# One sparse and one global attention stage of an eight-stage kernel: biases, rotary halves, row sums and start order moved between engines

## The reference

```python
# sparse, over the 2048 tokens
Q, K, V = (x @ W.T + b for each)            # 16 heads of 8
q_scores = 0.5*l2 + 0.3*entropy + 0.2*var   # of each row of Q, softmax over its 8 elements
_, top_idx = jax.lax.top_k(q_scores, 10)    # 10 queries a head
attn = softmax(Q_sparse @ K.T / sqrt(8)); out = attn @ V      # rows beyond u are dropped
return full.at[top_idx].set(out) @ Wo.T + bo
# global: 16 heads of 64, 4 key and value heads
q = q * cos + _rotate_half(q) * sin;  k = k * cos + _rotate_half(k) * sin
attn = softmax(q @ k.T * 64**-0.5);  out = attn @ v
return out @ Wo + bo
```

## Time and profile before

| | us |
|---|---|
| median of 3 runs (range) | 3885.16 (3882.11 to 3892.41) |
| the profiled execution, its own time | 3877.67 |
| its span, first to last instruction | 3875.9 |
| mean granted clock | 0.945 of full |
| busy in the span: PE, DVE, ACT, POOL | 3460.4, 2522.3, 1832.9, 1613.7 |

### The profile page before, as it was taken

How to read it: one execution, slowest core, us unless ns; L and a number is a source line. 1 busy time by engine, 2 the same in 40 slices (tenths; PEclk the granted TensorE clock), 3 DMA queues, 4 the chain that set the end, 5 groups by cost and what they waited for, 6 DMA issues and landing times. The chain is left out here.

```text
span 3875.9 us, 61610 instructions
## 1 busy us (share of the span) xinstructions
PE 3460.4 (89%) x23550; PEld 2161.1 (56%) x23550; DVE 2522.3 (65%) x4730; ACT 1832.9 (47%) x3269; POOL 1613.7 (42%) x1100
## 2 busy tenths in 40 slices
PE   6999999999857647999669999999999999978997
PEld 4777787878756435777523333333333333336776
DVE  4565656565655456777567777677677766757776
ACT  2344444434323124999423334333433333339997
POOL 1212121111104123666225556556655666656664
PEclk9999999999988557999879999999999999989999
DMA  2000000000010001000100000000000000010000
GB/s 94 1 1 1 1 1 1 1 1 1 1 45 9 6 0 44 2 2 2 38 0 1 1 1 1 1 1 1 1 1 1 1 1 1 1 44 2 2 2 12
DMA packets 21486, 31.46 MB, mean 8 GB/s; under 512 B 8418, under 2 KB 17932, under 8 KB 19724
## 3 DMA queue, kind: packets, MB, share of 16 engines
q1 hardware_dynamic: 21196, 27.52, 2.3%
HBM read 26.46 MB, written 1.05 MB: 7 GB/s over the span
## 5 line engine op out<-in xcount | busy, mean ns | idle before, releaser
L3027 POOL TENSOR_TENSOR global_acc_pool<-global_acc_pool,global_probs 128x1024 f32<-128x1024 f32 x320 | 776.7, 2427 | 470.6 <-ACT global_probs L2980 452.6
L2980 ACT ACTIVATE global_probs<-global_ps 128x1024 f32<-128x1024 f32 x512 | 524.7, 1025 | 883.2 <-PE global_ps L2853 856.9
L3075 DVE TENSOR_REDUCE global_part<-global_ps 128x2 f32<-128x1024 f32 x512 | 624.7, 1220 | 428.9 <-PE global_ps L2835 428.7
L2853 PE MATMUL global_ps<-global_q,global_k 64*128 64x512 f32 x2048 | 522.4, 588 | 0.0
L2864 PE MATMUL global_ps<-global_probs,global_v 128*64 128x512 f32 x2048 | 495.7, 605 | 0.0
L2835 PE MATMUL global_ps<-global_khh,global_qhh 64*128 64x512 f32 x1024 | 324.9, 631 | 35.9 <-DVE global_part L3075 33.9
L994 DVE COPY_PREDICATED delta_Y<-delta_tri,delta_ps 128x512 f32<-128x512 uint32 x192 | 140.4, 731 | 290.9 <-PE delta_ps L533 290.9
L900 POOL TENSOR_TENSOR delta_gm<-C_tile,delta_g 128x1024 f32<-128x1024 f32 x16 | 30.4, 1897 | 718.9 <-PE delta_ps L453 685.3
L2851 PE MATMUL global_ps<-global_mrow,global_first 64*128 64x512 f32 x1024 | 323.6, 629 | 0.0
L2864 PEld LDWEIGHTS global_ps<-global_probs,global_v 128*64 128x64 f32 x2048 | 124.3, 136 | 282.6 <-issue 161.4
L2835 PEld LDWEIGHTS global_ps<-global_khh,global_qhh 64*128 64x128 f32 x1024 | 97.9, 188 | 323.0 <-DVE global_part L3075 259.3
(11 more groups left out here) (587 smaller groups left out, 6862.3 us busy)
## 6 DMA issues: line engine op xcount, KB each, us to landing
delta_cw<-in_conv_taps SPq DMA_DIRECT2D x4, 1024.0 KB, 11.5
local_tab<-in_rot_tables SPq DMA_DIRECT2D x2, 2048.0 KB, 12.3
local_tab<-in_rot_tables SPq DMA_DIRECT2D x2, 1536.0 KB, 7.9
localw_wqkv<-in_L_ffn_wqkv SPq DMA_DIRECT2D x2, 768.0 KB
delta_wqkvz<-in_L_attn_a_W_qkvz SPq DMA_DIRECT2D x1, 1024.0 KB, 6.5
local_tab<-in_rot_tables SPq DMA_DIRECT2D x2, 512.0 KB, 4.2
global_cos<-in_rope_cos SPq DMA_DIRECT2D x2, 512.0 KB, 10.2
global_sin<-in_rope_sin SPq DMA_DIRECT2D x2, 512.0 KB, 11.7
```

Source lines behind the costliest of these rows:

```text
L2853: mm = pe.matmul(ps[:, 2 * (at % 2) + s, :], k2[own, group_of(u) % 2, P * k:P * k + P], q[own, u % 3, :], start=False, stop=True)
L2980: act.activation(probs[:, at % RING, :], ps[:, 2 * (at % 2):2 * (at % 2) + 2, :].rearrange("p b n -> p (b n)"), ACT.Exp).then_inc(S["probs ...
L3027: ins = eng.tensor_tensor(sums[:, u % 2, :], sums[:, u % 2, :], probs[:, at % RING, :], ALU.add)
L3075: dve.tensor_reduce(part[:, u % 2, r % SLOTS, :], ps[:, 5:7, :], X_AXIS, ALU.max)\
```

## The change

In the sparse stage the bias matmuls go, and DVE adds the biases of q and v while it copies them out of PSUM; ACT squares the copy; PE transposes a group ahead of each projection; the exponentials are interleaved with the copies. In the second block the probabilities stay unscaled, both halves are transposed before one series of 16 matmuls with 160 columns, and the inverse sums scale the output rows in the ACT copy.

In the global stage a rope key has one projection. ACT copies its halves of 32 partitions crosswise out of PSUM, with the sign (`swap_halves`, four activations of 32x512), and DVE multiplies the projection by cosine and the swapped copy by sine. The weights are loaded during the local stage before, the tables in four parts with a semaphore each. The first rope keys are interleaved with the rough scores of unit 0, which use two pairs of banks. POOL adds the two partial sums (`merge_sums`), so that `out_sums` has two matmuls for four. `out_sums`, the inversion, `out_rows` and the adding of rows each come one span later; POOL adds the output bias.

```diff
@@ -1819,21 +1819,20 @@
-                    def project(g, banks, i, bias):
+                    def project(g, banks, i):
                         for t in range(GROUP):
-                            own = ps[:, banks[g % 2], P * t:P * t + P]
-                            pe.matmul(own, xnT[:, g % 2, P * t:P * t + P], wT[:, i, :], start=True, stop=False)
-                            mm = pe.matmul(own, ones[0:1, :], bias[0:1, :], start=False, stop=True)
+                            mm = pe.matmul(ps[:, banks[g % 2], P * t:P * t + P], xnT[:, g % 2, P * t:P * t + P], wT[:, i, :],
+                                           start=True, stop=True)
                         return mm
...
+                    turn_rows(0)
+                    pe.wait_ge(S["wT_ready"], 1)
                     for g in range(GROUPS):
-                        turn_rows(g)
-                        if g == 0:
-                            pe.wait_ge(S["wT_ready"], 1)
+                        if g + 1 < GROUPS:
+                            turn_rows(g + 1)
                         project_all(g)
@@ -1867,24 +1867,26 @@
+                    def exponents(g):
                         act.wait_ge(S["shifted"], g + 1)
                         act.activation(e8[:, g], e8[:, g], ACT.Exp).then_inc(S["exp_ready"], 1)
+
+                    keep_rows(0)
+                    for g in range(GROUPS):
+                        if g + 1 < GROUPS:
+                            keep_rows(g + 1)
+                        keep_projections(g)
+                        if g:
+                            exponents(g - 1)
+                    exponents(GROUPS - 1)
@@ -1911,12 +1913,20 @@
+                        tiles = slice(GROUP * g, GROUP * g + GROUP)
+                        dve.wait_ge(S["q_ps"], g + 1)
+                        dve.tensor_tensor(q_all[:, tiles, :], ps[:, Q_BANKS[g % 2], :].rearrange("p (t d) -> p t d", t=GROUP),
+                                          over_middle(bq, GROUP), ALU.add).then_inc(S["q_ready"], 1)
+                        dve.wait_ge(S["v_ps"], g + 1)
+                        dve.tensor_tensor(v_all[:, tiles, :], ps[:, V_BANKS[g % 2], :].rearrange("p (t d) -> p t d", t=GROUP),
+                                          over_middle(bv, GROUP), ALU.add).then_inc(S["v_ready"], 1)
@@ -2003,28 +2013,27 @@
-                def contexts(g):
-                    pe.wait_ge(A["probsT_ready"], g + 1)
+                def contexts():
+                    pe.wait_ge(A["probsT_ready"], 2)
                     for t in range(TILES):
-                        mm = pe.matmul(ps[:, 4 * g + 3, 0:HALF], v_all[:, t, :], probsT[:, g, t, :],
+                        mm = pe.matmul(ps[:, 7, 0:H * TOP], v_all[:, t, :], probsT[:, :, t, :],
...
                 turn_probs(0)
-                contexts(0)
                 turn_probs(1)
-                contexts(1)
+                contexts()
@@ -2050,7 +2059,8 @@
-                    act.activation(ow[:, g, :], ps[0:HALF, 5 + g, 0:DIM], ACT.Copy).then_inc(A["ow_ready"], 1)
+                    act.wait_ge(A["weights_ready"], g + 1)
+                    act.activation(ow[:, g, :], ps[0:HALF, 5 + g, 0:DIM], ACT.Copy, scale=srow[:, g:g + 1]).then_inc(A["ow_ready"], 1)
@@ -2105,12 +2115,11 @@
                     link(dve.reciprocal(own, own))
-                    link(dve.tensor_tensor(own, own, valid[:], ALU.mult))
-                    dve.tensor_scalar(probs[:, g, :], probs[:, g, :], own, None, ALU.mult).then_inc(A["probs_ready"], 1)
+                    dve.tensor_tensor(own, own, valid[:], ALU.mult).then_inc(A["weights_ready"], 1)
...
-                own_heads(1)
+                row_weights(0)
+                row_weights(1)
+                dve.wait_ge(A["o_ps"], 1)
+                dve.tensor_tensor(oT[:], heads(ps[:, 7, 0:H * TOP], H), over_inner(hm, TOP), ALU.mult)\
...
+                load_global_weights(sp, C)
 
             @block.tensor
...
 
-    rope_order = [("k", 0, b) for b in range(QB)] + [("q", 0), ("q", 1)]
+    rope_order = [("q", 0)] + [("k", 0, b) for b in range(QB)] + [("q", 1)]
     for u in range(UNITS):
@@ -2787,52 +2829,56 @@
+                for b in range(QB):
+                    cols = slice(BLK * b, BLK * b + BLK)
+                    for half in (UP, DOWN):
+                        sp.dma_start(cos[half, cols], W["rope_cos"][:, cols]).then_inc(tables[b], 16)
+                        sp.dma_start(sin[half, cols], W["rope_sin"][:, cols]).then_inc(tables[b], 16)
+                sp.dma_start(wo[:], W["L1_attn_b_Wo"].rearrange("(c p) n -> p c n", p=P)).then_inc(S["wo_loaded"], 16)
...
-                pe.matmul(ps[:, 7, :], weights, xnT[:, cols], start=True, stop=True).then_inc(S["proj_ps"], 1)
+                    weights = wk[:, key[1], :, :].rearrange("d a e -> d (a e)")
+                pe.matmul(ps[:, proj_bank(n), :], weights, xnT[:, cols], start=True, stop=True).then_inc(S["proj_ps"], 1)
...
-                if r:
+                if r > SLOTS:
                     pe.wait_ge(S["max_done"], r)
+                elif r >= 2:
+                    pe.wait_ge(S["max_done"], r - 1)
+                first_bank = rough_banks(r).start
...
-                pe.wait_ge(S["sum_step"], (u + 1) * len(dve_adds))
-                pe.wait_ge(S["odd_step"], (u + 1) * (TILES - len(dve_adds)))
+                pe.wait_ge(S["merged"], u + 1)
...
-                for n, sums in enumerate((acc, acc_pool)):
-                    for s, own in enumerate((UP, DOWN)):
-                        mm = pe.matmul(ps[own, 7, :], ones[:, 0:HD], sums[:, u % 2, BLK * s:BLK * s + BLK],
-                                       start=(n == 0), stop=(n == 1))
+                for s, own in enumerate((UP, DOWN)):
+                    mm = pe.matmul(ps[own, 7, :], ones[:, 0:HD], acc_pool[:, u % 2, BLK * s:BLK * s + BLK],
+                                   start=True, stop=True)
...
+                for c in range(CHUNKS):
+                    for qt in range(QT):
+                        rough_scores(pe, QT * c + qt)
+                        if qt == 1:
+                            if c + 2 < CHUNKS:
+                                project(pe, ("k", 0, c + 2))
+                            elif c + 2 == CHUNKS:
+                                project(pe, ("q", 1))
+                            values(2 * c)
+                        if qt == 3:
+                            values(2 * c + 1)
...
-                        if j < 2 and u + 2 < UNITS:
+                        if j == 0 and u + 2 < UNITS:
                             pe.wait_ge(S["mrow_ready"], u + 1)
-                            project(pe, ("q", u + 2), j)
-                        if j == 4 and u:
+                            project(pe, ("q", u + 2))
+                        if j == 5 and u:
                             out_rows(pe, u - 1)
...
-                            project(pe, next_keys(u), j - 5)
+                            project(pe, next_keys(u))
...
+                        if j == 2 and u:
+                            out_sums(pe, u - 1)
                         if at + 1 + AHEAD < UNITS * SLOTS:
                             rough_scores(pe, at + 1 + AHEAD)
-                        if j == 1 and u:
-                            out_sums(pe, u - 1)
@@ -2962,6 +3015,17 @@
+                    for a in range(4):
+                        b = a ^ 1
+                        ins = act.activation(swapped[32 * a:32 * a + 32, :], ps[32 * b:32 * b + 32, proj_bank(n), :], ACT.Copy,
+                                             scale=1.0 if a % 2 else -1.0)
+                    ins.then_inc(S["swap_ready"], 1)
...
+                act.activation(wq[:], wq[:], ACT.Copy, scale=SCALE).then_inc(S["scaled"], 1)
...
+                        if j == 0 and u + 2 < UNITS:
+                            swap_halves(("q", u + 2))
+                        if j == 6 and next_keys(u):
+                            swap_halves(next_keys(u))
...
+                def merge_sums(u):
+                    pool.wait_ge(S["sum_step"], (u + 1) * len(dve_adds))
+                    pool.wait_ge(S["odd_step"], (u + 1) * (TILES - len(dve_adds)))
+                    pool.tensor_tensor(acc_pool[:, u % 2, :], acc_pool[:, u % 2, :], acc[:, u % 2, :], ALU.add)\
+                        .then_inc(S["merged"], 1)
+
...
+                pool.wait_ge(S["rows_loaded"], 32)
+                pool.wait_ge(S["xn_ready"], TILES // GROUP)
+                pool.tensor_tensor(X[:], X[:], over_middle(bo[:], TILES), ALU.add).then_inc(S["bias_added"], 1)
...
+                    if at % TILES == 1 and at >= TILES:
+                        merge_sums(at // TILES - 1)
+                    if at % TILES == 7 and at >= TILES:
                         normalize_context(at // TILES - 1)
...
+                    if n:
+                        dve.wait_ge(S["rope_ready"], n)
+                    dve.tensor_tensor(rot[:, 0, :], ps[:, proj_bank(n), :], cos[:, columns(key)], ALU.mult)\
```

(32 more changed lines are left out.)

231 lines of the change are left out of this document (121 added, 110 removed).

## The result

The changed kernel takes 3781.63 us (median of 4 runs, 3779.35 to 3791.99) where the kernel before takes 3884.28 (4 runs beside it, 3882.11 to 3892.41): a ratio of 0.9737, with a 95% interval of 0.9714 to 0.976. The forecast was 3739, with a range of 3712 to 3785. So 103 us of the forecast 146 came. The profiled execution has a span of 3780.1 us, 95.8 less than before.

What follows compares the result with a forecast made beforehand. PE was taken to bound the global units, chains the global start and sparse stage. 37 + 9 + 28 + 73 - 1 = 146 us less: 3731.7 for the profiled execution, 3739 for the median, range 3712 to 3785.

Steps and rivals of the forecast that it cites:

- port and queue: Rival, global units: merge, rotation and join delay DVE's maxima 1.1 us in 31 units, 34 less gain: 3773; chance 0.20.
- Sparse, first block: Sparse stage: fewer projection instructions without alternation, DVE adding biases; 37 us less, bounds 30 and 41.
- Sparse, second block: Sparse stage: first transposes beside the second exponential and one context series; 9 us less, bounds 4 and 12.
- Global start: Start of global stage: earlier tables, 5.0 us a rope key, back-to-back maxima; 28 us less, bounds 21 and 33.
- Units: Global stage's units: fewer projections and sum matmuls on PE, less new DVE delays; 73 us less, bounds 39 and 94.
- now both stand in one, 0.7 more: Global units, j = 0: both DVE rotation products in one span, 0.2 us lost in 30 units, 6 in all.
- The join in j = 7: Global units with keys: join ahead of place_max costs 0.85 us in 12 units, 10.2; net key gain 3.6.
- The wait of 8 us that was to go: Global units without keys, j = 5: PE's 0.4 us wait for DVE goes as out_rows comes between; 8 in 20 units.
- the bound of one blocked step a unit: Global units, lower bound 39: the merge blocks one DVE step for 1.1 us on PE's path in each of 31 units.
- The tail: End of global stage: a merge of some 2 us after the last add, 0.9 less of sums; 1 us more.
- The swap: Global units, j = 0: ACT's crosswise copies stay hidden; rival has them 1 us each, 3812, chance 0.05.
- The clock: Rival, global units: new gaps drop PE's clock to 0.50, some 42 us a unit; six units give 3991; chance 0.02.

Runs made afterwards that it cites:

- bias_on_pe: The changed kernel with the q and v biases added by 1-row matmuls on PE again, DVE only copying: 3814.22 us (one run).
- two_series: The changed kernel with the sparse stage's contexts as two successive series of 16 pairs of 80 columns: 3796.48 us (one run).
- pool_short: The changed kernel with GpSimd's adds and merge cut to 64 of 1024 columns (output not the reference's): 3700.35 us.
- before_pool_short: The kernel before the change with GpSimd's adds cut to 64 of 1024 columns (output not the reference's): 3874.66 us.
- join_early: The changed kernel with the key's join behind place_max and the query's join moved from j = 1 to j = 0, ahead of tile 15's add: 3761.21 us.
- rope_gpsimd: The changed kernel with the key's join behind place_max, and the sine product and both joins moved to GpSimd: 3729.79 us.
- norm5: 4adds with the normalization behind GpSimd's add of tile 5 in place of tile 6: 3723.95 us.
- 4adds: rope_gpsimd with DVE's add of tile 3 given to GpSimd and the normalization one tile earlier: 3763.02 us.
- no_merge: The changed kernel with merge_sums taken out and out_sums with its four matmuls again: 3793.87 us.

## Why the prediction was right, and where it was not

- **The sign and the range**: right, the time is 3 us inside the upper end, which was set by the rival "port and queue" (3773). That rival, with a chance of 0.20, is what happened; its price was 34 us, and 61 were lacking. That the time is still in the range is luck: the sparse stage and the start gave 17 us more than forecast, and 6.6 of these come through a clock that the forecast left low. Without the 17 the time would be some 3799, outside.
- **The signs of being wrong**: the prediction named waits of PE for `global_part` or `global_mrow` of over 1 us a unit, and a clock under 1.00 within the units. Both came: 62.2 us in 32 units, and the five stretches at 0.50.
- **Sparse, first block, 37 forecast, 41.4 measured.** The walk over DVE holds: from one group's first sum to the next (1324.43, 1330.65, 1336.87) it is 6.2 us, for 6.4 in the forecast. That PE would need 6.7 does not hold: from the second group on its 16 projections run at 0.12 us, not 0.22, at a clock of 1.00, where bias_on_pe, with the 1-row matmuls, stays at 0.50. DVE became the bound, earlier than forecast.
- **Sparse, second block, 9 forecast, 11.2 measured, and 6.6 more in the last product**, which the forecast left as it was, at the clock of before. two_series shows both.
- **Global start, 28 forecast, 31.6 measured.** DVE's table wait is gone, a key takes 5.2 us (swaps at 1857.66, 1862.86, 1868.06) for 5.0, and the sixteen maxima run back to back in fours. The first and the last four of them, and the first scores, in the timeline:

```profile
1872.48 4.61 DVE L3170 TENSOR_REDUCE global_part<-global_ps 128x2 f32<-128x1024 f32 x4
...
1892.04 4.61 DVE L3170 TENSOR_REDUCE global_part<-global_ps 128x2 f32<-128x1024 f32 x4
...
1906.50 0.79 PE L2897 MATMUL global_ps<-global_mrow,global_first 64*128 64x512 f32 x2
```

  The maxima end at 1896.65, 52.0 us behind the stage's start, for 54.8 in the forecast. The copies of 32 partitions took 0.59 each, as the row of 16.
- **Units, 73 forecast, 12.2 measured: the term that failed.** The work on PE was right: 34.5 + 32.6 + 13.8 = 80.9 us were to go, and pool_short is 1441.3 - 1357.8 = 83.5 shorter in them than before_pool_short. What was mis-sized is what the change costs on DVE. The step "now both stand in one, 0.7 more" took the sine product at the price of the product out of PSUM, though the change turns its operand from PSUM to SBUF; its mean was 1.365, and the two kinds of units paid 0.2 and 1.0. The join in j = 7 was charged 0.85 a unit with keys; it cost 1.7 of PE's time there and more behind it. `merge_sums` was taken at nothing on the ground that POOL has room and PE asks late, with the lock as a bound only; it cost 20 us. The wait of 8 us that was to go (9.0 measured) grew to 41.8 instead.
- **The chain of the argument that was missing**: the bound of one blocked step a unit was for one lock. In a unit without keys four are met by it (join, copy and two adds), by some 4.3 us together, in one with keys six or seven, by some 7; before, it was three and four, but two or three of these by 0.3 us or less, some 1.7 us together (each against its length in pool_short). What each costs is what it delays behind it, not its own length: in join_early the locks on join and add cost DVE less, and PE 1.02 us in j = 1, where the changed kernel waits 0.42 and 0.29.
- **The tail**: 1 forecast, 1.3 measured. **The swap** stayed hidden, as said.
- **The clock**: the rival had it falling for whole units, which did not happen. It fell for five stretches, 17.2 us together, behind waits of 1.7 us, where the longest wait for DVE in the units of before is 1.3.

For the row of an add at 2.30 us beside POOL's the prediction named the rule of the Trainium skill (SBUF — State Buffer, "SBUF: two separate sides"): a DVE step in a 2-port mode or with two inputs in SBUF and a GpSimd step can't both have the shared port pair; whichever starts first has it for its whole instruction, and the other blocks. The rows above agree in both directions: DVE's steps of 512 columns end 0.55 us behind POOL's, whether they began 0.8, 1.0 or 2.2 us into it, and POOL's add takes 3.34 us where DVE was 0.07 ahead. The rule was weighed as a rival and should have been a term, since it says which steps are met: the sine product, by the change, became one with two inputs in SBUF.

## What to carry to other kernels

When an edit moves an operand of a DVE step from PSUM to SBUF, or adds a step to GpSimd, look up in the trace which GpSimd step runs at that moment. In these traces the DVE step then cost the rest of that step plus nearly its own time, and what mattered was whether a result that the bound engine waits for stood behind it. Steps that need SBUF alone and are in no hurry did better on GpSimd, behind its own work (29 us in rope_gpsimd), but what its queue must deliver has to be moved forward with them (norm5 against 4adds, 39 us). And where a stage runs at the lower clock, ask of each edit what it does to the clock: here that was worth 6.6 of the 13.7 us of the one series.

## What the runs showed of the hardware that was not expected

- A DVE step of 512 columns with both operands in SBUF ended 0.55 us behind the GpSimd step that it met, one of 1024 columns 1.09 us behind it; a plain copy from SBUF to SBUF on DVE (tile 3) is met as well, 1.71 us on the mean where pool_short has it at 0.68. Reductions and products that read PSUM were not met (0.68 and 1.21 us throughout).
- PE's clock stayed at 0.50 while PE was busy for 27.96 of 28.2 us with instructions of 80 columns or of 80 rows (two_series), and for 56.4 of 57 us with 1-row matmuls in between (bias_on_pe); with 160 columns, and without the 1-row matmuls, it rose to 1.00. two_series and bias_on_pe ran once each.
- Of the twelve waits of 1.7 us in the units of the changed kernel, five were followed by a stretch at 0.50, and of the twelve in no_merge, one. Behind the twelve waits of 1.54 us in join_early the clock stayed at 1.00.
